# First four steps of the gate/up stage as plain block products, with the sums of x and of units 0 and 1 made later

## The reference, cut to what matters

```python
xn = layernorm(x)                     # x: 4 sequences x 1024 tokens x 1024 features
s  = attention over the 4 sequences, token by token (4x4 scores), plus xn
W  = NF4[codes] * scales              # gate, up: 2752 x 1024; down: 1024 x 2752; a scale per 64 inputs
g  = silu((silu(xn Wg^T) * (xn Wu^T)) Wd^T)
out = x + s * g
```

## Time and profile before

| | |
|---|---|
| median of 3 runs | 2463.22 us |
| profiled execution | 2463.08 us |
| its span, first to last instruction | 2461.3 us |
| mean granted TensorE clock | 0.99 of full |
| busy: TensorE, VectorE, ScalarE | 97%, 65%, 40% |

### The profile page before, as it was taken

How to read it: one execution, slowest core, us unless ns; L and a number is a source line. 1 busy time by engine, 2 the same in 40 slices (tenths; PEclk the granted TensorE clock), 3 DMA queues, 4 the chain that set the end, 5 groups by cost and what they waited for, 6 DMA issues and landing times.

```text
span 2461.3 us, 30006 instructions
## 1 busy us (share of the span) xinstructions
PE 2395.6 (97%) x11166; PEld 1103.2 (45%) x11166; DVE 1602.3 (65%) x2687; ACT 995.8 (40%) x1082; POOL 83.2 (3%) x71
## 2 busy tenths in 40 slices
PE   2899999999999999999999999999999999999999
PEld 2444444444444444444444444444444444444444
DVE  8888778668898877788888886565422432431432
ACT  8786777777878443444445422110010000001001
POOL 0000000000000000000000000000010011001011
PEclk6899999999999999999999999999999999999999
DMA  6855776656776885566655544248767767777764
GB/s 249 258 174 199 244 253 212 199 197 228 254 249 212 288 337 195 176 217 214 218 189 197 198 153 145 99 164 313 303 260 314 308 255 282 306 280 297 301 266 165
DMA packets 172414, 576.37 MB, mean 234 GB/s; under 512 B 17744, under 2 KB 44928, under 8 KB 154476
## 3 DMA queue, kind: packets, MB, share of 16 engines
...
## 4 chain that ended last, share of the span: by engine, by line
PE 92%; DVE 2%; DMA 2%; ACT 2%; issue 1%; SPq 0%; ACTq 0%; DVEq 0%
PE ps L1876 60%; PE ps L2036 32%; DMA arena<-in_x 1%; ACT arena L1019 1%; ACT arena L818 1%; PE ps L1827 1%; DMA arena<-xnsc 1%; DMA xnsc<-arena 0%; DVE arena L1400 0%; ACT arena L1009 0%; DVE arena L1380 0%; DVE arena L1354 0%; DVE arena L1392 0%; SPq L534 0%; DVE arena L1311 0%
## 5 line engine op out<-in xcount | busy, mean ns | idle before, releaser
L1876 PE MATMUL ps<-arena 128*128 128x512 f16 x7152 | 1552.2, 380 | 10.4 <-ACT arena L1025 7.5
L1876 PEld LDWEIGHTS ps<-arena 128*128 128x128 f16 x7152 | 699.5, 98 | 850.4 <-ACT arena L1025 7.9
L2036 PE MATMUL ps<-arena 128*128 128x512 f16 x3648 | 787.5, 379 | 0.0
L818 ACT ACTIVATE arena<-arena,bias_t 128x2048 f32<-128x2048 f32 (+3 forms) x288 | 525.0, 1829 | 75.2 <-DMA arena<-in_dn 66.8
L2036 PEld LDWEIGHTS ps<-arena 128*128 128x128 f16 x3648 | 356.9, 98 | 430.4
L1471 DVE TENSOR_TENSOR arena<-arena 128x512 f16<-128x512 f32 x364 | 244.1, 688 | 12.6 <-ACT arena L987 11.3
L1264 ACT ACTIVATE arena<-arena,e_d 128x512 f32<-128x512 f32 x48 | 34.6, 721 | 417.4 <-DVE arena L1792 219.4
L1035 ACT ACTIVATE arena<-ps,gate_back 128x512 f32<-128x512 f32 x84 | 57.1, 679 | 305.3 <-PE ps L1876 305.2
L787 POOL TENSOR_TENSOR arena<-arena 128x512 f32<-128x512 f32 x63 | 81.2, 1298 | 2357.5 <-DMA arena<-in_xt 2065.2
L1763 DVE SCALAR_TENSOR_TENSOR arena<-arena,sc 128x512 f32<-128x512 f32 x192 | 129.9, 746 | 0.0
L1045 ACT ACTIVATE arena<-arena,gate_back 128x512 f32<-128x512 f32 x84 | 60.4, 719 | 154.8 <-DVE arena L1644 144.9
...
## 6 DMA issues: line engine op xcount, KB each, us to landing
...
```

The source lines that it names most:

```text
L818: a_.activation(buf, src, ACT.Prelu, bias=bias_t[:, i:i + 1], scale=scale, alpha=alpha).then_inc(ramps, 1)
L1876: ins = t_.matmul(ps[:, bank, :], wreg[:, b, w, wa, k, :], xreg[:, j, o, k, xa, :], start=start and (k, wa, xa) == (0, 0, 0), stop=stop an ...
L2036: ins = t_.matmul(ps[:, bank, :], ring_w[b][:, k, wa, g, :], ring_i[b][:, k, xa, :], start=first and (k, wa, xa) == (0, 0, 0), stop=r not ...
```

## The change

Steps 0 to 3 are made as plain block products: each of the four result blocks (c11, c12 of the gate, c21, c22 of the up part) is the sum of two block products, 2 x 4 x 3 = 24 matmuls, so 96 a step. They need no sums. The order on TensorE is step 0, step 1, then steps 3 and 2 alternating by feature block.

Visits come in two kinds. A "plain" visit (e = 0 to 7) transposes the blocks straight from the tiles, now tiles 8 to 15 too (`half_tile` goes for these), copies them, makes high and low parts of the four blocks, and stores the blocks to HBM. A "sums" visit loads them again and makes the four sums, their high and low parts, for steps from 4 on. The block b12, which is none of the seven operands, stands for a while where sums go later (`B12_AT`), so the sums' high parts of visits 2 to 7 wait for products that still read it. Two more weight buffers hold the block (7) of units 0 and 1. Units 0 and 1 get their sums behind their plain blocks. The evaluations behind steps 0 to 3 are two Silu passes (`plain_silus`) and two gate multiplications (`plain_gates`). Normalization of tiles 12 and 13 moves from ScalarE to VectorE. A one-off Silu pass at the start makes the activation table be loaded there. `first_half(4)` now stands behind all of the above, and the first part of unit 3, on VectorE.

The core of the diff (empty lines and inner indentation reduced; removed lists of the engines' order are left out except SP's):

```diff
+NPLAIN = 4
+PLAIN = ["c11", "c12", "c21", "c22"]
+PLAIN_OPS = {"c11": [(0, 0), (1, 1)], "c12": [(0, 3), (1, 2)], "c21": [(7, 0), (3, 1)], "c22": [(7, 3), (3, 2)]}
+PLAIN_BANK = [4, 0, 0, 4]
+B12_AT = [[(3, 2), (3, 3), (4, 2), (4, 3)], [(3, 0), (3, 1), (3, 2), (3, 3)]]
...
-    if s < 2:
-        return half(s, FIRST, FIRST_REST) + half(s, SECOND, SECOND_REST)
+    if s < NPLAIN:
+        return [(t, n) for t in [[0], [1], [2, 3], []][s] for n in PLAIN]
...
-NORM_ACT = [5, 6, 7, 12, 13]
+VISITS = ([("plain", e) for e in range(4)] + [("sums", 0), ("sums", 1)] + [("plain", e) for e in range(4, 8)]
+          + [("sums", e) for e in range(2, 8)])
+VISIT = {c: i for i, c in enumerate(VISITS)}
+NG = 2
+NORM_DVE = [0, 1, 2, 3, 4] + list(range(8, 32))
+NORM_ACT = [5, 6, 7]
...
 def load_early(e):
-    for tt in range(8, 16):
-        sp.wait_ge(xs_out[nat_slot(tt)], 16)
-    sp.wait_ge(e_lo, NG * (e - 1))
-    sp.wait_ge(eb_out[e % 2], 64)
+    v = VISIT["sums", e]
+    if e == 3:
+        sp.wait_ge(et_done, 16)
+    else:
+        sp.wait_ge(e_lo, NG * (v - 2) + NG)
+    sp.wait_ge(eb_out[e % 2], 64 if e < 2 else 128)
     for r in (0, 1):
-        sp.dma_start(early[e % 2][:, r, :, :], xnsc[0, e - 4 + 4 * r, :, 2:4, :]).then_inc(eb_in[e % 2], 16)
+        sp.dma_start(visit_buffer(v)[:, r, :, :],
+                     xnsc[0, e % 4 + 4 * r, :, e // 4 * 2:e // 4 * 2 + 2, :]).then_inc(eb_in[e % 2], 16)
...
-store_early(0)
-store_early(1)
-store_xn(8)
-store_xn(9)
 load_scl(1, 0)
 load_scl(1, 1)
-store_early(2)
-store_xn(10)
-store_xn(11)
-store_early(3)
-for tt in range(12, 16):
-    store_xn(tt)
-load_early(4)
-load_early(5)
-for s in range(TOTAL):
+for e in range(4):
+    store_early(e)
+load_early(0)
+load_early(1)
+load_scl(2, 0)
+load_scl(2, 1)
+for e in range(4, 8):
+    store_early(e)
+for e in range(2, 6):
+    load_early(e)
+load_scl(3, 0)
+load_scl(3, 1)
+load_early(6)
+load_early(7)
+for o in X_ORDER:
+    store_stage(("i", 0, 0), o)
+load_stat(16)
+load_stat(17)
+for s in range(NPLAIN, TOTAL):
...
+def early_high(kind, e, g):
+    v = VISIT[kind, e]
+    if kind == "plain":
+        act.wait_ge(ee_done, 2 * e + g + 1)
+    else:
+        act.wait_ge(ep_made, 3 * e + (3 if g else 1))
+        if e in (2, 3):
+            act.wait_ge(prod, prod_at(1, "c22"))
+        elif e in (4, 5) and g:
+            act.wait_ge(part_made, e - 3)
+        elif e in (6, 7):
+            act.wait_ge(prod, prod_at(3, "c22"))
+    a_.activation(early_dest(v, g, 0), visit_buffer(v)[:, g, :, :], ACT.Copy).then_inc(e_hi, 1)
+def early_highs(kind, e):
+    early_high(kind, e, 0)
+    early_high(kind, e, 1)
...
+def plain_silus(s):
+    h, u, j = STEPS[s]
+    act.wait_ge(prod, prod_at(s, "c11"))
     if s:
+        act.wait_ge(ia_made, s)
+    a_.activation(silA, ps[:, PLAIN_BANK[s], :], ACT.Silu, scale=gate_back[:, u:u + 1]).then_inc(silA_made, 1)
+    act.wait_ge(prod, prod_at(s, "c12"))
+    if s >= 2:
+        act.wait_ge(ib_made, s - 1)
+    a_.activation(vB[s % 2], ps[:, PLAIN_BANK[s] + 1, :], ACT.Silu, scale=gate_back[:, u:u + 1]).then_inc(silB_made, 1)
...
+a_.activation(junk_s[:, :], bias_t[:, :], ACT.Silu)
...
+early_evac(0)
+w_high(0, (0, 1))
+early_highs("plain", 0)
+w_high(0, (3,))
+w_high(0, (7,))
+for e in range(1, 4):
+    early_evac(e)
+    early_highs("plain", e)
+for n in range(7, 16):
     ramp(1, n)
+early_highs("sums", 0)
+w_high(1, (0, 1))
+w_high(1, (3,))
+w_high(1, (7,))
+early_highs("sums", 1)
+plain_silus(0)
+w_high(0, (4, 5))
+w_high(0, (2, 6))
+early_evac(4)
+early_highs("plain", 4)
+store_w(0)
+load_codes(2)
+w_high(1, (4, 5))
+early_evac(5)
+early_highs("plain", 5)
+w_high(1, (2, 6))
+early_evac(6)
+early_highs("plain", 6)
+early_evac(7)
+early_highs("plain", 7)
+store_w(1)
+load_codes(3)
+for n in range(5):
+    ramp(2, n)
+plain_silus(1)
+early_highs("sums", 2)
+for n in range(5, 8):
+    ramp(2, n)
+early_highs("sums", 3)
+for n in range(8, 12):
+    ramp(2, n)
+early_highs("sums", 4)
+for n in range(12, 16):
+    ramp(2, n)
+early_highs("sums", 5)
+w_high(2, (4, 5))
+ramp(3, 0)
+w_high(2, (2, 6))
+for n in range(1, 5):
+    ramp(3, n)
+plain_silus(2)
+w_high(2, (0, 1))
+w_high(2, (3,))
+plain_silus(3)
+early_highs("sums", 6)
+early_highs("sums", 7)
...
+    if s == NPLAIN:
+        for n in range(5, 8):
             ramp(3, n)
...
+    b = visit_buffer(VISIT["sums", e])
+    dve.wait_ge(eb_in[e % 2], 32 * (e // 2) + 32)
+    v_.tensor_tensor(b[:, 0, :, :], b[:, :, 1, :], b[:, 0, :, :], ALU.subtract).then_inc(ep_made, 1)
     dve.wait_ge(ep_made, 3 * e + 1)
+    v_.tensor_tensor(b[:, 1, 1, :], b[:, 1, 1, :], b[:, 0, 0, :], ALU.subtract).then_inc(ep_made, 1)
     dve.wait_ge(ep_made, 3 * e + 2)
+    v_.tensor_tensor(b[:, 1, 0, :], b[:, 1, 0, :], b[:, 1, 1, :], ALU.subtract).then_inc(ep_made, 1)
+def early_low(kind, e):
+    v = VISIT[kind, e]
+    for g in (0, 1):
+        dve.wait_ge(e_hi, NG * v + g + 1)
+        v_.tensor_tensor(early_dest(v, g, 1), visit_buffer(v)[:, g, :, :], early_dest(v, g, 0), ALU.subtract).then_inc(e_lo, 1)
...
+def plain_gates(s):
+    h, u, j = STEPS[s]
+    ia, ib = (odd if u % 2 else even[j])
+    ub = up_back[:, u:u + 1]
+    b = PLAIN_BANK[s]
+    dve.wait_ge(prod, prod_at(s, "c21"))
+    dve.wait_ge(silA_made, s + 1)
+    v_.scalar_tensor_tensor(ia, ps[:, b + 2, :], ub, silA, ALU.mult, ALU.mult).then_inc(ia_made, 1)
+    dve.wait_ge(prod, prod_at(s, "c22"))
+    dve.wait_ge(silB_made, s + 1)
+    v_.scalar_tensor_tensor(ib, ps[:, b + 3, :], ub, vB[s % 2], ALU.mult, ALU.mult).then_inc(ib_made, 1)
...
+for i in (0, 1):
+    scaled(0, i)
+for tt in (8, 9):
+    normal(tt)
+w_low(0, (0, 1))
+early_low("plain", 0)
+w_low(0, (3,))
+w_low(0, (7,))
+for tt in (10, 11):
+    normal(tt)
+early_low("plain", 1)
+for tt in (12, 13, 14, 15):
+    normal(tt)
+early_low("plain", 2)
+early_low("plain", 3)
 early_sums(0)
+early_sums(1)
+scaled(1, 0)
+scaled(1, 1)
+early_low("sums", 0)
+for ops in PLAIN_W:
+    w_low(1, ops)
+early_low("sums", 1)
+def parts_of(u):
+    tg, tu = yb[2 * (u % 2)], yb[2 * (u % 2) + 1]
+    return tg[:, 0:512], tg[:, 512:1024], tu[:, 0:512], tu[:, 512:1024]
+w_sum(0, 0, parts_of(0))
+w_sum(0, 1, parts_of(0))
+plain_gates(0)
+w_low(0, (4, 5))
+w_sum(0, 2, parts_of(0))
+w_sum(0, 3, parts_of(0))
+w_low(0, (2, 6))
+w_sum(1, 0, parts_of(1))
+w_sum(1, 1, parts_of(1))
+early_low("plain", 4)
+w_low(1, (4, 5))
+w_sum(1, 2, parts_of(1))
+w_sum(1, 3, parts_of(1))
+early_low("plain", 5)
+w_low(1, (2, 6))
+early_low("plain", 6)
+early_low("plain", 7)
+early_sums(2)
+plain_gates(1)
+early_low("sums", 2)
+early_sums(3)
+early_low("sums", 3)
+early_sums(4)
+early_low("sums", 4)
+for i in range(4):
+    w_item(2, i)
+early_sums(5)
+w_item(2, 4)
+w_item(2, 6)
+w_item(2, 7)
+early_low("sums", 5)
+w_low(2, (2, 6))
+for i in range(9):
+    c_item(("i", 0, 0), i)
+plain_gates(2)
+w_low(2, (0, 1))
+w_low(2, (3,))
+for i in range(9, len(JOB_ITEMS)):
+    c_item(("i", 0, 0), i)
+plain_gates(3)
+early_sums(6)
+early_low("sums", 6)
+early_sums(7)
+early_low("sums", 7)
+for i in range(4):
+    w_item(3, i)
+for s in range(NPLAIN, TOTAL + 1):
+    if s - 2 >= NPLAIN:
...
+        if e == 4 and r == 0:
+            pe.wait_ge(silA_made, 1)
+            pe.wait_ge(silB_made, 1)
+        elif e == 4:
+            pe.wait_ge(ia_made, 1)
+            pe.wait_ge(ib_made, 1)
...
+    if s == NPLAIN and name in FIRST:
+        pe.wait_ge({"p1": silA_made, "p7": silB_made, "p5": ia_made, "p6": ib_made}[name], 3)
+    elif s == NPLAIN + 1 and name in FIRST:
+        pe.wait_ge({"p1": q_made, "p7": silA_made, "p5": silB_made, "p6": ia_made}[name], 1 if name == "p1" else 4)
     elif name == "p1":
...
+def plain(s, k, names=PLAIN):
     h, u, j = STEPS[s]
+    for name in names:
+        bank = PLAIN_BANK[s] + PLAIN.index(name)
+        if k == 0 and s == 0:
+            pe.wait_ge(sct_evac, 6)
+        elif k == 0 and s == 1:
+            pe.wait_ge(ee_done, 8)
+        elif k == 0 and s == 3:
+            pe.wait_ge(ee_done, 16)
+        elif k == 0:
+            pe.wait_ge({"c11": silA_made, "c12": silB_made, "c21": ia_made, "c22": ib_made}[name], 2)
+        if k == 0 and j == 0:
+            pe.wait_ge(w_lo, w_done(u, (0, 1) if name in ("c11", "c12") else (7,)))
+        if name == "c11":
+            pe.wait_ge(e_lo, NG * VISIT["plain", 4 * j + k] + NG)
+        for n, (w, o) in enumerate(PLAIN_OPS[name]):
+            o, at = B12_AT[j][k] if o == 3 else (o, k)
             for wa, xa in TERMS:
+                wt = a21[u][:, wa, k * P:(k + 1) * P] if w == 7 else wreg[:, wbuf(0, u), w, wa, k, :]
+                ins = t_.matmul(ps[:, bank, :], wt, xreg[:, j, o, at, xa, :], start=(k, n, wa, xa) == (0, 0, 0, 0),
+                                stop=(k, n, wa, xa) == (3, 1, 1, 0), skip_group_check=True)
+        if k == 3:
+            ins.then_inc(prod, 1)
+        elif s == 2 and name == "c22" and k < 2:
+            ins.then_inc(part_made, 1)
+plain(0, 0)
+early_transposes(2)
+plain(0, 1)
```

(87 more changed lines are left out.)

347 lines of the change are left out of this document (113 added, 234 removed).

## The result

The kernel with the change took 2497.21 us in the median of four runs (2495.01 to 2498.47), the one before 2463.1 beside it (2462.55 to 2463.6): ratio 1.0138, 95% interval 1.0120 to 1.0155. That is slower by 34 us. The profiled execution took 2497.26 us and its span 2495.5: +34.2 on the span, where +28.5 was forecast.

What follows compares the result with a forecast made beforehand. Before step 6 the nearly full helpers VectorE and ScalarE hold TensorE, which bounds the rest. Instructions placed behind their waits, stretch by stretch, start p1 of step 6 28.5 us later: 2463.1 + 28.5, median 2491.7 us; range 2464 to 2504.

Steps and rivals of the forecast that it cites:

- Start: Up to the first plain product: copies, high and low parts let it begin at 48.2 us, after about 3 us of standstill.
- Step 0: From 48.2 to 74.8 us: 96 matmuls 20.8, 32 transposes 3.8, a restart 2.0; VectorE and ScalarE keep up.
- The gap before step 1: TensorE waits for unit 1's low parts behind sums and loads: stands 11.8 us, restarts for 2.0.
- Step 1: From 86.6 to 117.0 us: matmuls 20.8, transposes 4 x 1.9, a restart 2.0, the helpers just ahead.
- Steps 3 and 2: Up to 159.6 us: load 2 lands at 121.7, 1.0 us of standstill for gates, then 41.6 us of matmuls without a wait.
- Before step 4: VectorE waits four times, unit 2's low part comes at 165.6 us: TensorE stands 6.0 and restarts, 2.0.
- Before step 5: Largest standstill: q comes at 192.2 us, behind unit 3's ramps on ScalarE; TensorE stands 14.2 and restarts, 2.0.
- Before step 6: Unit 4's codes, issued at 192.5 us, and ramps hold ScalarE: p1 starts at 216.4 instead of 187.9, +28.5.
- The loads are slower: Rival: doubled HBM block traffic makes visits 1 and 2 1.3 + 3.0 us later each, +9 to +11: 2502; chance 0.11.
- The helpers never wait behind the second gap: Rival: from 125.8 us loads, ramps and high parts are always ready, +11.6 us: 2475; chance 0.17.
- VectorE stays as full as now: Rival: VectorE stands still only 12.4 us up to q of step 4, so faster: 2457.9 us; chance 0.10.
- The change moves nothing: Rival: helpers' work bounds both kernels, VectorE idle 17.6 +- 5 us, time within 4.9 us of now; chance 0.08.

Runs made afterwards that it cites:

- e1: Changed kernel with unit 1's two scaled passes, three low parts and three high parts put ahead of the sums of visits 0 and 1: 2497.72 us.
- e2: Changed kernel with plain_gates(1) put ahead of early_sums(2) on VectorE, so the gates don't stand behind load 2: 2496.71 us.
- e4: Changed kernel with 48 matmuls of the plain steps left out, 84 a step as in the kernel before, result less exact: 2495.16 us.
- e6: Changed kernel with the first four items of unit 3 on VectorE put behind q of first_half(4): 2496.67 us.
- e9: Kernel before with only the small Silu pass at the start, which loads the activation table there: 2462.99 us against 2463.22.
- e3: Changed kernel with unit 1's weight store and unit 3's codes load put behind the high parts of sums visit 2: 2493.15 us.
- e10: Changed kernel's work reordered: all plain visits before all sums visits, with codes, ramps, gates, unit 1's blocks, staging and q moved too: 2479.5 us.

## Why the prediction was right, point by point

| step of the forecast | predicted | measured | off by |
|---|---|---|---|
| Start: first product | 48.2 | 47.53 | -0.7 |
| Step 0: its end | 74.8 | 73.58 | -1.2 |
| The gap before step 1: `plain(1, 0)` | 86.6 | 85.55 | -1.0 |
| Step 1: its end | 117.0 | 114.9 | -2.1 |
| Steps 3 and 2: load 2 landed | 121.7 | 129.2 | +7.5 |
| the same: their end | 159.6 | 168.2 | +8.6 |
| Before step 4 | 165.6 | 172.66 | +7.1 |
| Before step 5 | 192.2 | 198.85 | +6.7 |
| Before step 6 | 216.4 | 222.03 | +5.6 |

(The end of step 1 is 18 of the 42 matmuls of the row at 110.98, at 0.217; the rest of the row is the first block of step 3.)

(The row of load 2 is VectorE's start behind it.)

**The mechanism held.** TensorE began 20 us sooner and had no use of it, since no helper had less to do (e1, e2, e4 and e6: what is taken from TensorE's waits or work comes back as a later wait). The largest standstills came where the forecast put them, before steps 1 and 5, with 11.96 and 13.25 us for 11.8 and 14.2, released by a weight's low part and by q; the wait for the ramp was 5.21 us for 5.4. Beside the 11.96 us the profile names no releaser ("issue"); by time it is the first of the low parts at 84.23, which ends at 85.5, and e1, which moves them forward, moved the start by 5.7 us. The table load brought nothing that can be seen (e9). Behind p1 of step 6 the two traces differ by a shift, as forecast, but in part by luck: the sum has neither the restart behind the 3.58 us nor the later waits of the kernel before, and these are 1.6 and 1.2 us more.

**One term was mis-sized, in *Steps 3 and 2*.** I took 6.3 us from issue to landing for load 2; it took 14.8 from its first issue at 114.44 to VectorE's start. The mistake was to price a load by its like in the trace of before and not by what is issued around it: in the same paragraph store 7 stands in front of it on SP's queue, and in ScalarE's list a weight store and a codes load are moved to the same microsecond. e3 takes two of them away and the load lands 6.0 us sooner. So of the rival *The loads are slower* one event came true at more than its price (+7.5, where +4.3 per visit was given), and the other, visit 1's, not at all: it landed in time for 77.10. By the number this is near: the measured 2497.2 lies 5.5 us above the forecast and 4.8 below that rival's 2502, and 0.8 inside the 2483 to 2498 that carried the 0.54. The median of the loads, 5.5 us, is shorter than before (6.1). That stores of the same queue ran beside the loads in the trace of before, as the forecast has it, isn't so: the last of those stores was issued at 82.5 us and landed 10.1 later, at 92.6, and the first load was issued at 92.8. The Trainium skill (DMA: Bandwidth & Descriptors, section "Anatomy of one DMA — SWDGE (gpsimd) path") fits one DMA of that path, where these loads go by a queue that the profile calls hardware_dynamic, with about 2 us plus its bytes at 436 GB/s. An estimate by it is 3.2 us for one load of 0.5 MB and 4.4 for a visit's two as one. The single loads here took 3.6 us at the fastest, 5.5 in the median and 13.9 at the longest, so the measurement decides, and the fit is no guide where queues meet.

**Two standstills more than forecast, off the path.** Between the end of step 1 and that of step 2, TensorE stood 3.56 us twice where 1.0 was placed, and its matmuls took 4.4 us more than 0.217 each, where no restart was placed: together 10.5 us, behind a start that was 2.1 us early, which is the +8.6 of the row to 0.2. The first standstill was released by `plain_silus(1)`, which stands behind the ramps that began 2.01 us late, the second by the gates behind load 2. They did not count by themselves: before step 4 TensorE waited for VectorE in any case, and e2, which takes the second away, gained nothing.

**From there the error shrank, by 3 us up to step 6.** VectorE's waits between 133 and 170 us came to 7.1 for 7.3 placed. The standstills before steps 4, 5 and 6 were 1.5, 1.0 and 0.4 us under their forecast, since TensorE came late to them as well.

**The helpers never wait behind the second gap** (2475) fell: VectorE waited for a ramp 5.2 us and for load 2. **VectorE stays as full as now** (2457.9) fell clearest: up to q of step 4 (36 to 198.1 us), the stretch of its 17.6 and of the 40 of my placing, it stood still 48.9 us, 41.4 of them before 164. Most of the 8.9 above the placing is load 2. **The change moves nothing** fell with it.

**What e4 adds.** The forecast carried 10.4 us for 48 more matmuls as a term of the sum. As a price it is right, on the path it mostly is not: without them only some 2 us come back, because each standstill behind step 1 ends when a helper is done, however early TensorE arrives. All that TensorE has more of busy time, restarts included, is 16.7 us, half of the loss, and that it is busy longer doesn't make it the cause of that half; only a sum by stretches, each ended by the engine that comes last, comes near the whole.

**Open.** Whether any order of this scheme beats the kernel before was not shown. e10 has 29.7 us of standstills (3.35, 4.97, 12.59, 7.38, 1.43) and the 10.4 us of products, against 16 us that are missing, so an order would have to win more than half of the standstills. VectorE's amount of work doesn't forbid it by these rows: it is busy 94 of 128 us there, and was busy 115.6 in the kernel before.
